# Attention's last tiles normalized and turned in another way, and two changed orders in the last stages

## The reference, cut to what matters

```
x = layernorm(x + L0_attn(x))   # gated linear attention, 16 heads of 16
x = layernorm(x + L0_ffn(x))    # 8 experts, top 2 by x @ router, and a shared expert
x = layernorm(x + L1_attn(x))   # keys, values, gradient of a 2-layer MLP over all tokens,
                                # one AdamW step on W1, W2, then the MLP on the queries
x = layernorm(x + L1_ffn(x))    # ternary weights, 256 -> 1024 -> 256
```

## Time and profile before

| | us |
|---|---|
| three runs | 1439.64, 1444.31, 1451.77; median 1444.31 |
| the profiled execution | 1432.45 |
| its span | 1430.7 |
| PE busy | 1340.5 (94%) |
| DVE busy | 796.7 (56%) |
| ACT busy | 580.0 (41%) |
| POOL busy | 303.7 (21%) |

### The profile page before, as it was taken

How to read it: one execution, slowest core, us unless ns; L and a number is a source line. 1 busy time by engine, 2 the same in 40 slices (tenths; PEclk the granted TensorE clock), 3 DMA queues, 4 the chain that set the end, 5 groups by cost and what they waited for, 6 DMA issues and landing times. The chain is left out here.

```text
span 1430.7 us, 22481 instructions
## 1 busy us (share of the span) xinstructions
PE 1340.5 (94%) x7683; PEld 851.2 (59%) x7685; DVE 796.7 (56%) x1539; ACT 580.0 (41%) x1280; POOL 303.7 (21%) x345
## 2 busy tenths in 40 slices
PE   7999999889998999999999997899999998899995
PEld 4556666655555666666666664456555663577774
DVE  5999999945441222222222221477777665676764
ACT  5577777550110222222222221334443532466665
POOL 2133333313660000000000003422220000244353
PEclk8999999989999999999999999999999999999998
DMA  5555666656220111111111113212110000000001
GB/s 205 205 199 202 201 218 199 202 186 233 93 101 10 44 44 44 44 44 44 44 47 48 44 44 107 70 30 88 30 30 0 1 0 12 0 1 16 30 16 59
DMA packets 76741, 115.83 MB, mean 81 GB/s; under 512 B 10032, under 2 KB 62576, under 8 KB 72560
## 3 DMA queue, kind: packets, MB, share of 16 engines
q1 hardware_dynamic: 70096, 97.89, 20.5%
q0 software_dynamic: 6144, 16.79, 3.7%
q10 hardware_dynamic: 416, 0.03, 0.0%
HBM read 82.86 MB, written 31.82 MB: 80 GB/s over the span
## 5 line engine op out<-in xcount | busy, mean ns | idle before, releaser
L1703 POOL DMA_INDIRECT m_got<-outs,slot x64 | 61.2, 956 | 560.9 <-DMA outs<-XT 451.2
L1108 DVE TENSOR_TENSOR ro_h<-ro_bB,ro_sl 128x512 f32<-128x512 f32 x71 | 49.1, 691 | 217.3 <-PE ro_bB L1057 217.3
L551 DVE TENSOR_TENSOR_SCAN a_dcy<-a_gbc,a_ident 128x2048 f32<-128x2048 f32 x32 | 142.5, 4452 | 5.9 <-DMA a_gbc<-gd 2.0
L2059 POOL TENSOR_TENSOR q_hr<-q_hf,q_hr 128x512 fp32r<-128x512 f32 x64 | 83.9, 1322 | 287.7 <-ACT q_hr L1900 287.7
L1052 PE MATMUL ro_bA<-Win,ro_xT 128*128 x284 | 134.6, 596 | 0.8 <-ACT ro_xT L1079 0.6
L1064 PE MATMUL ro_bO<-Wout,ro_hT 128*128 x568 | 134.3, 379 | 0.9 <-DVE ro_hT L1101 0.9
L1064 PEld LDWEIGHTS ro_bO<-Wout,ro_hT 128*128 128x128 f32 x568 | 107.8, 190 | 45.6 <-issue 34.6
L1057 PE MATMUL ro_bB<-Wsw,ro_xT 128*128 x284 | 133.4, 592 | 0.0
L1088 ACT ACTIVATE XT<-ro_bO 128x256 f32<-128x256 f32 x71 | 27.2, 383 | 204.9 <-PE ro_bO L1064 204.9
L1101 DVE COPY ro_hT<-ro_bH 128x512 f32<-128x512 f32 x71 | 49.1, 691 | 101.3 <-PE ro_bH L1037 101.3
L1057 PEld LDWEIGHTS ro_bB<-Wsw,ro_xT 128*128 128x128 f32 x284 | 54.0, 190 | 67.9 <-issue 67.9
(11 more groups left out here) (270 smaller groups left out, 2519.4 us busy)
## 6 DMA issues: line engine op xcount, KB each, us to landing
a_gbc<-gd SPq DMA_DIRECT2D x32, 1024.0 KB, 6.0
rows<-a_zero SPq DMA_DIRECT2D x8, 1152.0 KB, 9.2
XT<-rows SPq DMA_DIRECT2D x71, 128.0 KB, 2.0
outs<-XT SPq DMA_DIRECT2D x71, 128.0 KB, 1.7
a_xt<-in_xTt SPq DMA_DIRECT2D x8, 512.0 KB, 5.8
X<-in_x SPq DMA_DIRECT2D x8, 512.0 KB, 4.1
Win<-in_w_in SPq DMA_DIRECT2D x8, 512.0 KB, 10.6
Wsw<-in_w_sw SPq DMA_DIRECT2D x8, 512.0 KB, 10.4
```

The lines of the kernel that those rows point to most:

```text
L551: v.tensor_tensor_scan(dcy[:, :], gbc[j % 2][:, :], ident16[:, :], 0.0, ALU.mult, ALU.add).then_inc(d_done, 1)
L1703: pool.indirect_dma_start(out=got[q % 2][k][:, t, :], out_offset=None, in_=mem["outs"], in_offset=bass.IndirectOffsetOnAxis(ap=slot[:, k, ...
L2059: pool.tensor_tensor(hr[:, 1, f % 4, :], hf[f % 2][:, :], hr[:, 0, f % 4, :], ALU.subtract).then_inc(hl_done, 1)
```

## The change

In attention, tiles 24 to 27 (`PACED` = 24 on) leave the paced pipeline. DVE normalizes all four in step 31 behind the residual of tile 30 (`normalize_last`). TensorE turns them in two pairs in step 32, ahead of and behind the last `project_out`, into two banks of `bS` (`turn_last`); ACT copies each pair at once (`keep_last`); after the loop TensorE routes all four into a third bank (`route_last`) and one ACT copy takes the scores. The loop ends with n = 32 instead of 36. Moments of tiles 29, 30 and 31 are no longer taken in attention but by ACT at the head of the shared block, ahead of the first Silu; POOL there waits for the last of them before its scales. In memory's tail `grad1(7)` moves ahead of `queries(3)`. In the last block ACT's copy of projection 7 moves behind `normalize(0)`.

```diff
-        FIRST, LAST, SP_OPS = -5, NT + 5, 14
+        FIRST, LAST, SP_OPS = -5, NT + 1, 14
         KEPT = NT - 4
+        PACED = KEPT - 4
+        x4_done, t4_ready, t4_read, r4_ready = sem("x4_done"), sem("t4_ready"), sem("t4_read"), sem("r4_ready")
...
+        def paced(j):
+            return 0 <= j < PACED
...            # TensorE
+                def turn_last(h):
+                    pe.wait_ge(a_done, 2 * NT)
+                    for k in range(2 * h, 2 * h + 2):
+                        pe.wait_ge(x4_done, k + 1)
+                        for g in range(G):
+                            c = (k % 2) * D + g * P
+                            mm = pe.transpose(bS[:, h, c:c + P], X[:, PACED + k, g * P:(g + 1) * P], ident[:, :])
+                    mm.then_inc(t4_ready, 1)
+
+                def route_last():
+                    for k in range(4):
+                        pe.wait_ge(t4_read, k // 2 + 1)
+                        for g in range(G):
+                            mm = pe.matmul(bS[:, 2, k * E8:(k + 1) * E8], XT[:, g, (PACED + k) * P:(PACED + k + 1) * P], Wr[:, g, :],
+                                           start=(g == 0), stop=(g == G - 1))
+                    mm.then_inc(r4_ready, 1)
...
+                    if n == NT:
+                        turn_last(0)
                     if tile(n - 1):
                         project_out(n - 1)
+                    if n == NT:
+                        turn_last(1)
...
-                    if carries(n - 9):
+                    if paced(n - 9):
                         router(n - 9)
...
-                    if carries(n - 8):
+                    if paced(n - 8):
                         turn_x(n - 8)
...
+                route_last()
...            # ACT
+                def keep_last(h):
+                    act.wait_ge(t4_ready, h + 1)
+                    act.activation(XT[:, :, (PACED + 2 * h) * P:(PACED + 2 * h + 2) * P].rearrange("p g (t c) -> p t g c", t=2),
+                                   bS[:, h, :].rearrange("p (t g c) -> p t g c", t=2, g=G), ACT.Copy).then_inc(t4_read, 1)
...
-                    elif carries(n - 9):
+                    if n == NT:
+                        keep_last(0)
+                        keep_last(1)
                         act.wait_ge(r_ready, n - 8)
...
-                    if tile(n - 2):
+                    if 0 <= n - 2 <= KEPT:
                         moments(n - 2)
-                    if carries(n - 7):
+                    if paced(n - 7):
                         normalize(n - 7)
+                act.wait_ge(r4_ready, 1)
+                act.activation(mem["score"][:, PACED:KEPT, :], bS[:, 2, 0:4 * E8].rearrange("p (t e) -> p t e", e=E8), ACT.Copy)
...            # DVE
+                def normalize_last():
+                    T = PACED // 4
+                    v.wait_ge(sh_done, T + 1)
+                    for k in range(4):
+                        v.tensor_scalar(X[:, PACED + k, :], X[:, PACED + k, :], rstd[T % 2][:, k:k + 1], shift[T % 2][:, k:k + 1],
+                                        ALU.mult, ALU.add).then_inc(x4_done, 1)
...
                         residual(n - 1)
+                    if n == NT - 1:
+                        normalize_last()
...            # shared block, ACT
+                late = mem["mv"][(NC - 1) % 2]
+                for k in range(1, 4):
+                    if k > 1:
+                        act.wait_ge(lv_done, k - 1)
+                    act.activation(sl[1][:, 0:D], X[:, LATE + k, :], ACT.Copy, scale=-1.0 / D, accum_out=late[:, k, 0:1]).then_inc(lm_done, 1)
+                    act.wait_ge(lm_done, k)
+                    act.activation(sl[1][:, 0:D], X[:, LATE + k, :], ACT.Square, bias=late[:, k, 0:1], accum_out=late[:, k, 1:2]).then_inc(lv_done, 1)
+                act.wait_ge(lv_done, 3)
...            # shared block, POOL
+                pool.wait_ge(lv_done, 3)
...            # memory's tail, TensorE
                 turn_dz1(q)
+                grad1(q)
                 pe.wait_ge(td2_read, 2 * NB)
                 queries(3, pair(q + 1, Z2))
-                grad1(q)
...            # last block, ACT
-                    if q == 1:
-                        queries(7, 2, bH)
                     if block_of(q - 4):
                         finish(q - 4, 0, 2)
...
                     if block_of(q - 1):
                         normalize(q - 1)
+                    if q == 1:
+                        queries(7, 2, bH)
```

More of the change, by code:

```diff
@@ L381, in _ @@
                             pe.wait_ge(sig_done, min((n + 4) // 4 + 1, NC))
-                        if carries(n - 10):
+                        if paced(n - 10):
                             pe.wait_ge(r_read, n - 9)
@@ L706, in build_shared_and_routes @@
         LATE = NT - 4
+        lm_done, lv_done = sem("lm_done"), sem("lv_done")
         bR = bank("bR")
```

## The result

The changed kernel takes **1434.18 us** (median of 14 runs, 1428.53 to 1439.98); the kernel before, run beside it, 1445.86 (14 runs, 1439.64 to 1451.77). The ratio is **0.9921, 95% interval 0.9906 to 0.9936**: 11.4 us less (9.3 to 13.6), where the sum said 11.8. It is within 1% of no change.

A forecast was written before the change was run, and what follows sets the result against it. TensorE was taken to bound the kernel from the shared block on, with engine hand-overs in attention's tail. Part 1 -6.9, part 2 -0.7 and part 3 -4.2 sum to -11.8 us from the 1444.31 median: 1432.5 us, range 1421 to 1442.

The forecast's parts named there:

- Part 1, tail: Attention's tail: four tiles normalized, turned, copied and routed together move the block's end from 300.35 to 292.8, -7.55 us.
- the low end: Attention's tail: with a low clock over route_last, the 16 router matmuls take about twice 1.8 us, leaving -5.7.
- signs of being wrong: up(2) later than 11.5 after the block's start, a POOL or DVE tail wait above 1 us, or a downstream gap.
- Part 1, bill: Shared block: 3.4 us of moments hidden, -0.2; low clock over up(2) after idling 2.3, half of 1.76 taken, +0.8.
- Part 2: Memory's tail: grad1(7) ahead of queries(3) gives -0.7 us, from an earlier block end and the clock.
- The direct term: Memory's tail: the block ends 0.2 us earlier, not 1.5, because ACT's copy of the last query is late next.
- The clock term: first(0), last block: TensorE's gap ahead shrinks from 3.47 to 1.85; -0.5 us taken, bounds -1.76 and +1.7.
- Part 3: Last block: second(1) starts 2.7 us earlier and runs 1.55 faster, -4.2; sign: under 1.2 us behind projection 7.
- That low stretch stays: Last block: the gap of 3.42 behind second(1) and the low clock after it (5.29) stay.
- the kind clock: Rival: low stretches at first(0), up(2) and first(2) vanish or hide, -15.6 us in all, 1428.7; chance 12%.
- table-load rival: Shared block: Silu table load ahead of the moments on ACT costs 1.28 us, -10.5 in all, 1433.8; chance 12%.
- rival of the slow clock over up(2) to up(5): Shared block: 1.2 GHz through up(5) and the first down costs 21 us, whole +9, 1453.5; chance 4%.

The follow-up runs named there:

- clean pair: Profiled executions of the kernel before and of the unchanged changed kernel, profiled again in the first series of experiments; spans 1430.7 and 1416.3 us.
- after_again: The changed kernel, unchanged, measured again beside the three parts alone, against the kernel before: 1418.84 us, ratio 0.9916.
- moments_twice: The changed kernel with the three late moments computed twice at the shared block's head: 1437.14 us, ratio 0.9936 to the kernel before.
- p1_attention: The kernel before with only attention's tail and the moved moments changed; memory's tail and last block as before: 1423.83 us, ratio 0.9945.
- filled_w1: The kernel before plus three unused matmuls on TensorE in memory's tail, during its wait for DVE's update of W1: 1442.58 us, ratio 0.9983.
- first series: Experiments measuring each part of the change alone and the whole again; the kernel before, run beside them, had a median of 1431.04 us.

## Why the prediction was right

The forecast was 1432.5; the median is 1434.18, the saving 11.4 for 11.8. Three measurements of the same kernel give 11.4, 12.0 and 13.3. The mechanism of each part is the one forecast. That the sums come so near is partly luck: in the clean pair the bill of part 1 came out 0.75 us better than forecast, the stretch behind part 3 1.23 worse, and within part 2 two effects of 1.7 and 1.1 us cancel in the main. Two of these terms are a matter of chance in each execution, as the traces show: the clock half of part 3 (1.7) and the stretch behind it.

- **Part 1, tail: -7.55 forecast, -7.6 found** (13.47 to 5.89 between the last attend and the next block; 13.22 to 13.47 in the five traces with the old tail, 5.88 to 6.05 in the nine with the new one). The steps hold one by one: four normalizes 1.38 (1.2 as taken), 16 router matmuls 1.93 (1.8), last copy at 292.7 (292.8). A low clock over them, the low end, came in none of the nine. Of the signs of being wrong, a DVE wait above 1 us in the tail, one was just touched: 0.80 and 0.77 us here, 1.01 in after_again, without cost.
- **Part 1, bill: +0.6 forecast, -0.15 found.** The chain was right (3.5 us of moments, load behind them, up(2) at 10.09 for 10.1), the clock wrong: TensorE idles 1.23 ahead of the late turns and some 0.9 between them (1.92 for what takes 1.04 at full clock), near my 2.3, but no trace of the changed kernel has a low stretch on up(2). moments_twice shows that the danger was real, at 4.75 of idle. The price that I halved was also misread: 1.76 us is not the dearest low stretch of these rows, since the first four matmuls of the earlier trace rows alone took 3.75 for 1.88.
- **Part 2: -0.7 forecast, -0.95 in the clean pair.** The direct term was right (-0.2, found -0.36: an ACT copy now ends the block). The clock term (-0.5) is -1.69, and there in all nine traces with the new order. What I had not named is the load of the query weights behind first(0): its cover was the low clock itself, and 0.7 to 1.1 us of it now show, so the net, -0.6, is near the term by luck.
- **Part 3: -4.2 forecast, -4.08 found**, as wait 2.4 and clock 1.7, where I had 2.7 and 1.55. second(1) starts 1.13 behind the end of projection 7, under the 1.2 named as a sign. The clock half was a chance of this one trace of before: against p1_attention or filled_w1, where second(1) is at full clock, the same part is worth 2.4.
- **Behind part 3: 0 forecast, +1.23 in the clean pair.** "That low stretch stays" was right as to its being there in most traces (8 of 12), not as to its size: 4.22 to 5.73 on first(2), and in four of the six unfilled traces with all three parts the turns are slow as well (1.97 for 1.09). From turn_h(1) to the first ternary matmul it is 3.97 to 6.93 in these six, 3.96 to 5.66 in the six others without fillers there. So the +1.23 may be the scatter of one pair; that the change brings it isn't shown.
- **The profiled time**: I took it for an outlier of 11.9 below the runs, with the gaps the same in them. Those runs have no trace. What the traces show is that it is an execution without the two stalls, and that every trace of a slower series has both; the ratio is the same with and without.
- **Two sums** behind the range and the chances are off, without bearing on the time: 1428.7 to 1436.4, widened by half of the spread (6.1), is 1422.6 to 1442.5, not 1421 to 1442, and the kind clock with a quarter of the forecast is 0.26, not 0.29.

The table-load rival fell: the load stands at 296.46, directly before the first Silu, as the earlier trace rows had it, and it stands there in all nine traces with part 1. The Trainium skill ("ScalarE activation tables: per-element evaluation and per-set limits", on table sets in the compiler and the runtime) states that the back end places the loads per block by greedy longest run. The trace disagrees with what I took from that, a load ahead of the moments, and not with the rule itself: the Copy and Square passes of the moments ran with the load that attention had made at 232.32. The rival of the slow clock over up(2) to up(5) fell too: even moments_twice lost only 1.0 us on the first four matmuls of up(2), and the next four took 1.88.

## What to carry to other kernels

- Where the last items of a paced pipeline drain one by one through three engines, take them off it together: one engine normalizes, pairs are turned and copied, one run of small matmuls serves all. Here it is two thirds of the gain, and its size could be forecast from the rows to 0.1 us.
- A wait on TensorE costs its length and, in some executions or in all, a low stretch behind it. Count both, take the second from several traces and not from one, and look for what that low stretch was covering, since it comes into view when the clock stays up (here a load, 0.7 to 1.1 us).
- Before two traces are compared by their spans, measure the distances between fixed points of one engine's list. Two equal spans here hid 12 us of gain (the rows of the table that the change touches, first trace, the shared block left out) behind 12 us of stalls and scatter.

## What the runs showed of the hardware

- The clock behind a gap of one length is not one thing. Behind 3.47 us of TensorE idle the next eight matmuls took 5.17 to 6.58 in 4 of 4 traces; behind 3.42, 4.22 to 5.73 in 8 of 12 and 3.60 in 4; behind 1.93, 5.15 or 5.29 in 2 of 4 and 3.60 in 2; behind 1.61, 3.67 in 9 of 9. Behind 1.23, ahead of up(2), it never fell in the six traces that have such a wait (1.23 to 1.26) there; behind 4.75 it fell (2.90 for 1.88), in the one trace. With the time filled by unused matmuls it was 3.60 to 3.67 in all four traces, but only at the gap of 3.47 is that more than the unfilled ones show by chance. The places differ in what runs ahead of them, too, and no run parts that from the length.
- The same kernel took 1431.0 in one series and 1446 to 1448 in others, and in the slower ones every trace lost time in the shared block between 380 and 425 (38.06 to 43.17 us of TensorE busy, of 45), in the trace shown with TensorE and DVE waiting for "issue", and again at the head of the memory block (TensorE waits 5.83 to 8.94 us). All traces of the first series, and that of the kernel before, have 45.0 and 1.73. The ratios of the changed kernel agree all the same (0.9921, 0.9916, 0.9908). What the engines wait for in either place wasn't tried.
